# Token blocks of an attention and expert kernel: the fourth scores, the fourth mask and the decayed keys and queries take other places in four hand-written orders

## What is computed

```python
q, k, v = proj(Wq, bq), proj(Wk, bk), proj(Wv, bv)        # of layernorm(x); 16 heads of 32
alpha = 0.9 * sigmoid(silu(x @ Wg1 + bg1) @ Wg2 + bg2) + 0.1
scores = where(causal, q @ k.T / sqrt(D), -inf)           # within chunks of 64 tokens
intra = softmax(scores) @ v
def step(S, inp):                                         # a recurrence over all tokens
    inter_t = q_t @ S
    S = a_t[..., None] * S + k_t[..., None] * v_t[..., None, :]
x = x + inter + intra
x = x + moe(layernorm(x)) # router over 64 experts, top 8, capacity 256, plus a shared gated MLP
```

## Time and profile before

| | |
|---|---|
| median of three runs | 4699.62 us |
| the profiled execution | 4707.31 us |
| its span, first to last instruction | 4705.4 us |
| TensorE matmul busy | 4477.3 us, 95% |
| VectorE busy | 3518.8 us, 75% |
| ScalarE busy | 2271.9 us, 48% |
| GpSimd busy | 1334.0 us, 28% |
| mean granted TensorE clock | 0.982 |

### The profile page before, as it was taken

How to read it: one execution, slowest core, us unless ns; L and a number is a source line. 1 busy time by engine, 2 the same in 40 slices (tenths; PEclk the granted TensorE clock), 3 DMA queues, 4 the chain that set the end, 5 groups by cost and what they waited for, 6 DMA issues and landing times. The chain is left out here.

```text
span 4705.4 us, 183217 instructions
## 1 busy us (share of the span) xinstructions
PE 4477.3 (95%) x74416; PEld 3897.4 (83%) x74416; DVE 3518.8 (75%) x7639; ACT 2271.9 (48%) x7475; POOL 1334.0 (28%) x1275
## 2 busy tenths in 40 slices
PE   6999999999999999999999999999999969999998
PEld 5888888888888888888888888888888859999998
DVE  5777777777777777777777777777777768888887
ACT  4444444444444444444444444444444436666665
POOL 2111111111111111111112121211111146666666
PEclk9999999999999999999999999999999979999999
DMA  2000000101000000000000000001000069999997
GB/s 66 31 31 31 31 31 31 36 31 36 28 34 31 31 31 31 31 31 31 31 31 31 31 31 31 31 31 35 31 31 31 31 207 268 270 268 265 267 271 193
DMA packets 195054, 358.52 MB, mean 76 GB/s; under 512 B 16736, under 2 KB 92896, under 8 KB 194352
## 3 DMA queue, kind: packets, MB, share of 16 engines
q1 hardware_dynamic: 160848, 269.47, 16.9%
q0 software_dynamic: 33632, 79.73, 7.8%
HBM read 243.87 MB, written 107.50 MB: 75 GB/s over the span
## 5 line engine op out<-in xcount | busy, mean ns | idle before, releaser
L589 ACT ACTIVATE PR<-PR,MX 128x64 f32<-128x64 f32 x2048 | 682.6, 335 | 811.6 <-DVE MX L1171 811.6
L475 POOL TENSOR_TENSOR RI<-PV,AL 128x512 f32<-128x512 f32 x65 | 78.5, 1208 | 2540.0 <-DVE PV L1125 2540.0
L727 PE MATMUL bank<-XTh,wsguh 128*128 128x256 f32 x1536 | 447.0, 291 | 0.0
L1663 PE MATMUL ebank<-XH,WH 128*128 128x256 f32 x1536 | 431.2, 281 | 6.8 <-DVE XL L1745 6.8
L728 PE MATMUL bank<-XTl,wsguh 128*128 128x256 f32 x1536 | 430.4, 280 | 0.0
L729 PE MATMUL bank<-XTh,wsgul 128*128 128x256 f32 x1536 | 430.4, 280 | 0.0
L1663 PE MATMUL ebank<-XH,WL 128*128 128x256 f32 x1536 | 429.7, 280 | 0.0
L1663 PE MATMUL ebank<-XL,WH 128*128 128x256 f32 x1536 | 429.5, 280 | 0.0
L589 ACT ACTIVATION_READ_ACCUMULATOR PR<-PR,MX 128x1 f32 x2048 | 383.0, 187 | 0.0
L1738 DVE TENSOR_TENSOR WL<-WS,WH 128x768 fp32r<-128x768 f32 (+1 forms) x455 | 370.5, 838 | 16.2
L1600 ACT ACTIVATE WH<-WS 128x768 fp32r<-128x768 f32 (+1 forms) x455 | 325.3, 747 | 26.3 <-DMA WS<-in_L_ffn_w_down_dram 26.3
(11 more groups left out here) (228 smaller groups left out, 13456.6 us busy)
## 6 DMA issues: line engine op xcount, KB each, us to landing
WS<-in_L_ffn_w_gate_dram SPq DMA_DIRECT2D x65, 768.0 KB
WS<-in_L_ffn_w_up_dram SPq DMA_DIRECT2D x65, 768.0 KB
WS<-in_L_ffn_w_down_dram SPq DMA_DIRECT2D x65, 768.0 KB
norm_rows<-XR SPq DMA_DIRECT2D x64, 576.0 KB, 3.1
X<-in_L_attn_x_dram SPq DMA_DIRECT2D x66, 512.0 KB, 3.6
out_dram<-X SPq DMA_DIRECT2D x64, 512.0 KB, 2.9
CR<-token_counts,count_at POOLq DMA_INDIRECT x136
XG<-norm_rows,row_at POOLq DMA_INDIRECT x132, 6.4
```

Source lines behind the costliest of these rows:

```text
L475: nc.gpsimd.tensor_tensor(inverse[:, :, 0:half], PV[:, :, :], running[:, :, HC:half:-1], ALU.mult).then_inc(folded.sem, 1)
L589: ins = nc.scalar.activation(PR[b][:, j, :], PR[b][:, j, :], ACT.Exp, bias=MX[b][:, j:j + 1], scale=1.0, accum_out=SU[b][:, j:j + 1])
L727: nc.tensor.matmul(out, sh, mh, start=first, stop=False)
L1663: last = nc.tensor.matmul(bank[HID[m]][:, a * CAP:(a + 1) * CAP], w, x[odd][:, c, :], start=(c == 0 and i == 0), stop=(c == KC - 1 and i = ...
```

## The change

Nothing is added to the arithmetic or taken from it. Four orders are changed, and one wait is new.

- **TensorE:** `scores(t, 3)` goes ahead of the first half of the second key product, `turn_probs(t, 2)` too; the value chunks are joined (two ahead of `outputs(t, 2)`, four in one piece for tile 1); both halves of `x2t`, then `router`, then both tiles of `ktok` stand together.
- **VectorE:** `softmax_a(t, 3)` and `weights(t, 2)` go ahead of `inverse(n, 1)`; `residual(t, 0)` goes behind `weights(t, 3)`; `norm2(t, 0)` goes behind `residual(t, 1)`.
- **ScalarE:** `ot(t, 2)` goes ahead of `k_evac(n, 1)`, `lt` ahead of `ktok_evac(n, 0)`.
- **GpSimd:** both `rstd2` go ahead of `decayed_k`, and a new wait for both norms (`x2n_ready`) stands between.
- `BANK_OF` names `RL` ahead of `KTok0`; their banks stay.

```diff
--- before.py
+++ after.py
@@ -63,7 +63,7 @@
 
 
 BANK_OF = {"G1": 3, "Qa": 0, "G2a": 2, "G2b": 3, "Ka": 0, "Qb": 1, "Kb": 2, "ATr0": 3, "V0": 0, "V1": 1, "ATr1": 2,
-           "X2Ta": 3, "X2Tb": 0, "KTok0": 2, "RL": 1, "KTok1": 3, "GU0": 2, "RLT": 1, "GU1": 0, "GU2": 3, "DK": 1,
+           "X2Ta": 3, "X2Tb": 0, "RL": 1, "KTok0": 2, "KTok1": 3, "GU0": 2, "RLT": 1, "GU1": 0, "GU2": 3, "DK": 1,
            "DN0": 2, "DN1": 0}
 JOBS = list(BANK_OF)
 PROJECT = ["G1", "Qa", "G2a", "Qb", "G2b", "Ka", "Kb", "V0", "V1", "KTok0", "KTok1", "DK"]
@@ -522,10 +522,11 @@
                     t = Turn(pair, odd)
                     unpair(t.next())
                     fold(t.next())
+                    rstd2(t, 0)
+                    rstd2(t, 1)
+                    pool.wait_ge(x2n_ready.sem, t.value(x2n_ready))
                     decayed_k(t.next())
-                    rstd2(t, 0)
                     decayed_q(t.next())
-                    rstd2(t, 1)
                     rstd1(t.next(2))
 
 
@@ -682,12 +683,12 @@
                     q_evac(n, 1)
                     ot(t, 1)
                     exp(t, 3)
+                    ot(t, 2)
                     k_evac(n, 1)
-                    ot(t, 2)
                     ot(t, 3)
                     x2t(t)
+                    lt(t)
                     ktok_evac(n, 0)
-                    lt(t)
                     ktok_evac(n, 1)
                     gu(t, 0)
                     hidden_high(t, 0)
@@ -1018,25 +1019,23 @@
                     turn_probs(t, 1)
                     project(t, 1, wq, q_filled, ("Qa", "Qb"), parts=(1,))
                     outputs(t, 1)
+                    scores(t, 3)
+                    turn_probs(t, 2)
                     project(t, 1, wk, k_filled, ("Ka", "Kb"), parts=(0,))
-                    scores(t, 3)
                     turn_out(t, 0)
-                    values(t, 0, chunks=(0,))
-                    turn_probs(t, 2)
+                    values(t, 0, chunks=(0, 1))
+                    outputs(t, 2)
                     project(t, 1, wk, k_filled, ("Ka", "Kb"), parts=(1,))
-                    outputs(t, 2)
-                    values(t, 0, chunks=(1,))
                     turn_probs(t, 3)
                     values(t, 0, chunks=(2,))
                     outputs(t, 3)
                     values(t, 0, chunks=(3,))
                     turn_out(t, 1)
-                    values(t, 1, chunks=(0, 1))
+                    values(t, 1)
                     x2t(t, 0)
-                    values(t, 1, chunks=(2, 3))
                     x2t(t, 1)
+                    router(t)
                     ktok(t, 0)
-                    router(t)
                     ktok(t, 1)
                     gate_up(t, 0)
                     turn_logits(t)
@@ -1337,15 +1336,15 @@
                     weights(t, 1)
                     inverse(n, 0)
                     softmax_b(t, 2)
-                    inverse(n, 1)
                     softmax_a(t, 3)
                     weights(t, 2)
-                    residual(t, 0)
+                    inverse(n, 1)
                     softmax_b(t, 3)
                     weights(t, 3)
-                    norm2(t, 0)
+                    residual(t, 0)
                     values(n, 0)
                     residual(t, 1)
+                    norm2(t, 0)
                     norm2(t, 1)
                     values(n, 1)
                     x2t_low(t)
```

## The result

The changed kernel takes 4781.76 us (median of four runs, 4776.36 to 4788.3). The kernel before takes 4700.82 (four runs made beside them). The ratio is 1.0174, with an interval of 1.0156 to 1.0191: 1.7% slower. The forecast was 4753 with a range of 4705 to 4790. The sign and the range held; 29 us, or 0.45 us a block, are missing from the sum. That the range held is in part luck of where the code lies (experiments 10 to 12). The profiled execution took 4779.52 us with a span of 4777.7; before these were 4707.31 and 4705.4. The granted clock is the same within a thousandth (0.981, before 0.982), so the clock is not where the time went between these two kernels.

The account below looks back on a forecast made before the run. TensorE was taken to set the block (matmuls busy 54.96 of 55.92 us). The terms moved `gate_up(t, 0)` from 2025.32 to 2026.15, +0.83 us a block, +53 us over 64 blocks: 4753 us, range 4705 to 4790.

Parts of the forecast that it names:

- Step 1: TensorE from the second key product to the fourth outputs: 9.48 us after 10.06 before, a lead of 0.58 a block.
- Step 2: VectorE's fourth `PR` meets GpSimd's `unpair` and is held, but the fourth turn is not delayed: 0.
- Step 3: GpSimd's power for tile 1 is held by VectorE's `norm2(t, 0)`: 0.25 us, so the lead shrinks to 0.33.
- 4, `x2t` to router: TensorE from second `x2t` to the router's end: fixed 1.28 and 1.52 us, so the 0.33 lead is kept.
- Step 5: Late `decayed_k`, then the copy of `KTok0` no longer covered by the router, delay `gate_up(t, 0)`: 1.16 us a block lost.
- Step 6: Work queued behind GpSimd's new wait, up to the shared MLP's first product, has about 1.8 us of cover: no cost.
- late instructions: Rival: with outputs and scores adjacent, TensorE loses a further 0.3 us a block, giving 4772 us; chance 0.10.
- `PR` is held longer: Rival: VectorE's `PR` waits out further GpSimd work, +1.7 us a block (4811) or +4.0 (4955); chance 0.09.
- The rival in which the copy costs nothing: `gate_up` does not wait for the `KTok0` copy: +0.02 us a block (4701); chance 0.15, shared with a larger lead.
- would show it: Trace signs: fourth outputs at 9.5 us, second `norm2` 0.3 earlier, `rstd2` 0.8, `KD` 0.5 behind `norm2`, `KTok` wait, `PR` up to 1.8.

Follow-up runs that it names:

- experiments 10 to 12: Idle semaphore additions put ahead of TensorE's loop: changed kernel with 192 (4828.16 us), kernel before with 128 (4695.22 us) and with 192 (4725.87 us).
- (4): Changed kernel with VectorE's second reciprocal, `inverse(n, 1)`, moved behind `softmax_b(t, 3)`: 4782.57 us.
- Experiment 3: Changed kernel with the banks of `GU0` and `GU1` exchanged: 4744.53 us, ratio 1.0094.
- (7): Changed kernel with GpSimd's order of before: decayed keys ahead of the first power, decayed queries ahead of the second, no wait for the norms: 4881.2 us.
- (10): Changed kernel with 192 semaphore additions, run once ahead of TensorE's loop to shift its code: 4828.16 us, ratio 1.0255.
- (1): Changed kernel with 128 semaphore additions, run once ahead of TensorE's loop to shift its code: 4787.81 us, ratio 1.0189.

## Why the prediction was right, and where its sum was off

| step | forecast, us a block | measured |
|---|---|---|
| 1, lead up to the fourth outputs | -0.58 | -0.56 where no stall stands |
| 2, `PR` beside `unpair` | 0 | 0 (4) |
| 3, hold of `rstd2` | +0.25 in all blocks | 0.29 in places 1 and 3, mean +0.14 |
| 4, `x2t` to router | 0 | about 0 |
| 5, `ktok` behind the router | +1.16 | +1.12 (block 34), +1.05 (block 33) |
| 6, behind GpSimd's wait | 0 | 0 |
| late instructions | 0, a rival with +0.3 | 1.1 in two of four blocks, mean +0.55 |
| sum | +0.83 | about +1.2 |

**Step 1** held in its terms and failed in one assumption, that products follow one another as soon as data is there. In places 2 and 4 the stretch is what was laid out. In 1 and 3 the stall eats twice the lead. The rival "Instructions come late" named this very place, outputs and scores side by side, and got a chance of 0.10 and a price of 0.3; its argument against, that outputs and key products ran without such a loss in block 33, was true of products that use instructions more slowly. This is the term that was mis-sized. 0.83 and 0.55 for supply, less 0.11 for the hold and less 0.08 for the copy, makes 1.19, the growth of the mean block. The forecast is thus right in sign, in the steps and by its range, but the range was met by luck of the place: it ended 90 us above the kernel before. At shift 0 the orders differ by 81 us. At 64, 128 and 192 they differ by 0.0216, 0.0207 and 0.0210, which is 97 to 102 us and beyond it.

**Step 2.** What it expected is in the timeline, VectorE then GpSimd, block 33:

```profile
2045.44 0.20 DVE L1180 RECIPROCAL RU<-SU 128x8 f32<-128x8 f32 x1
2045.68 1.74 DVE L1181 TENSOR_TENSOR PR<-PR,RU 128x512 f32<-128x512 f32 x1
...
2045.67 1.20 POOL L475 TENSOR_TENSOR RI<-PV,AL 128x512 f32<-128x512 f32 x1 [41.43 <-DVE PV L1124]
2046.83 1.67 POOL L477 TENSOR_TENSOR RI<-PV,AL 128x512 f32<-128x512 f32 x1
```

`PR` ends at 2047.42, 0.55 behind the end of L475 (2046.87), within the 0.28 to 0.69 of the forecast. L477 had started ahead of that end and was not served: `PR` got its turn between two GpSimd instructions, and L477 then took 1.67 for 1.22. The rival "`PR` is held longer" falls with that. What was not foreseen is that this is a draw: in blocks 34 and 36 `PR` is first, takes 0.69, and L475 takes 1.74, hence its mean of 1498 ns on the page of the profile. The Trainium skill, "SBUF — State Buffer", section "Who interferes with whom", has both (the pair excludes each other for one instruction, and the issue order decides who blocks); the trace agrees, with 1.74 on either side.

**Step 3.** GpSimd's power for tile 1 and VectorE's norms, block 33, answer to the earlier trace rows:

```profile
2055.11 0.55 DVE L1211 TENSOR_SCALAR XR<-X,mv,rs 128x512 f32<-128x512 f32 x1
2056.09 0.55 DVE L1211 TENSOR_SCALAR XR<-X,mv,rs 128x512 f32<-128x512 f32 x1 [0.44 <-POOL rs L455]
...
2055.23 0.83 POOL L455 TENSOR_TENSOR rs<-ve,neg_half 128x1 f32<-128x1 f32 x1 [2.60 <-DVE ve L1204]
2057.06 2.37 POOL L512 TENSOR_TENSOR KD<-KT,RI 128x1024 f32<-128x1024 f32 x1 [1.00 <-DVE XR L1211]
```

The power starts 0.12 behind the norm and takes 0.83, not 0.54: the hold exists and was taken at the right size. In places 2 and 4 it starts nearer (2112.41, with both norms joined from 2112.35) and takes 0.54. A start 0.06 behind passes, in all 32 cases; one of 0.10 to 0.12 is held, in all 32 cases. The forecast had no means to see that.

**Step 5** is right in mechanism and near in size. `KD` starts 0.42 behind the end of `norm2` (2056.64 to 2057.06; forecast 0.5), takes 2.37, and `gate_up` comes 0.06 behind the end of the copy (2060.24 + 0.59 = 2060.83, then 2060.89; forecast 0.15). Experiment 3 took the bank's part out and got 37 us back. The rival in which the copy costs nothing falls. **Step 6** held: TensorE has no wait behind `gate_up` that it had not before, and the new order on GpSimd is worth 93 us (7).

What "would show it" named: fourth outputs at 9.5 us behind the old place of the key product, second norm 0.3 earlier, TensorE idle for `KTok`, `PR` at up to 1.8. No block has all of it. The fourth outputs come at 10.80 - 1.29 = 9.51 where nothing stalls, in places 2 and 4, and the second norm ends there 0.56 earlier behind the second outputs (16.85 for 17.41), more than the 0.33 of the forecast, because in these blocks the power is not held. The power at 0.83 and `PR` at 1.74 stand in places 1 and 3, where the stalls turn the lead into a lag. `KD` at 0.42 to 0.44 behind `norm2` and the wait for `KTok` are in all.

**Open.** The traces tie the stalls to pages that land late, and the order to the stalls. How far ahead TensorE fetches, and why one shift stalls more at the jump than another, was not tried. Blocks of place 1 without a stall take 56.74 (10) and 56.78 us (1) with the new order, 55.97 to 56.37 at the four shifts with the old one: +0.4 to +0.8, at or under the forecast of +0.83. The order costs 1.3 to 1.6 us a block in all (81 to 102 us). Of that 0.5 to 0.6 are the stalls of the table above, and the clock behind them is up to another 0.5. The parts of this sum were read from traces and not taken away one by one, apart from the bank's wait (3).

## What to carry to other kernels

Where TensorE sets the time and its products are small, count instructions, not only microseconds: 320 of them in 2.65 us, with no longer products between, were enough here for stalls of 1.1 us, and an edit that puts two such groups side by side has to be charged with that. A stall can also cost more than its own length, as in 7 and 10, where the clock fell behind it. Before a difference of under 1% between two orders is believed, run both at several shifts of the code. When a copy is moved off its cover, look at once for the bank that its reader and the next job share; another bank gave back half of this loss.

## What the runs showed of the hardware

- A page of instructions is one packet of 16,384 bytes (564 packets and 9.24 MB on q8 in the kernel after; 474 of them between 500 and 3700 us, one for every 242 of TensorE's matmuls and weight loads there). Its transfer took 0.9 to 1.4 us in nine cases of ten (kernel after). In 433 stalls of over 0.35 us in fourteen traces the work that stood resumed 1.16 to 1.62 us behind a landing, in the middle 1.4, and 2.2 to 3.4 behind the start of that transfer. Outputs and scores are 160 products with as many loads in 2.65 us; by the 242 this uses up a page in an estimated 2.0 us, faster than one comes. The Trainium skill, "Runtime: NRT & Kernel Launch", section "Instruction fetch mechanics", gives pages of 256 instructions, fetched ahead, and calls the cost of a crossing mostly hidden. The size of the packet agrees; the hiding does not hold here, where stalls of 0.4 to 2.7 us stand ahead of products with nothing else to wait for. The measurement decides.
- The granted clock fell to its lower level, 1.2 GHz, behind such stalls: behind 1.67 and 2.46 us of idle time at the jump of the kernel before (0.50 from 2157.98 to 2164.81), and in 7 behind one of 1.19 us in block 33. The stall of 1.11 us in block 33 of the kernel after was not followed by a fall.
- 64, 128 or 192 instructions that run once ahead of a loop changed the time of 64 blocks by -0.76% to +0.45% in the one kernel and by -0.3% to +0.8% in the other.
- `PR` of VectorE and L475 of GpSimd met within 0.06 us of each other in each block of the kernel after, and one was always held: 1.74 us for VectorE's product (0.69 alone) or 1.74 for GpSimd's (1.2 alone), according to which started first, be it by 0.01 us. The short power of GpSimd beside VectorE's norm passed at 0.06 us behind its start and was held at 0.10 to 0.12. The product that waits is served when the running instruction ends, even if the next is already queued.
- `KD` starts 0.42 to 0.44 us behind the norm that it waits for, with four more waits ahead of it whose counts are there; L475, with two waits, started 0.21 us behind its last one in the kernel before.
